# A four-layer graph network on one Trainium2 core: the score products of layer A in rounded halves, the column vectors of layer G by rows, and new steady sequences

## What is computed

```python
def layer_A(x, adj, Wq, Wk, Wv, Wo, bo):          # L0: masked attention, 4 heads of 64
    q, k, v = heads(x @ Wq), heads(x @ Wk), heads(x @ Wv)
    sim = where(adj, (q @ k.T) * 64 ** -0.5, -max)
    return merge(softmax(sim) @ v) @ Wo + bo
def layer_G(h, adj, W, bW, attn, A_w, ...):       # L1: 4 heads of 256
    Wh = h @ W[head].T + bW[head]
    scores = (Wh @ attn[head]) @ Wh.T
    hp = relu(tanh(where(adj, scores, 0)) @ Wh)
    ha, hf = concat(hp) @ A_w.T, h @ fc_w.T
    c = sigmoid(hf @ g1_w.T + ha @ g2_w.T + gbias)
    return hf * c + ha * (1 - c)
layer_B = ...                                     # L2: 8 heads of 32, scores and cosines
layer_D = ...                                     # L3: the same form as layer_A
x = norm(x + A(x)); x = norm(x + G(x)); x = norm(x + B(x)); x = norm(x + D(x))
```

## Time and profile before

| | |
|---|---|
| runs | 2783.31, 2783.71, 2779.02 us; median 2783.31 |
| profiled execution, its own time | 2784.76 us |
| its span | 2782.9 us |
| mean granted TensorE clock | 0.982 |
| share of the span that PE, DVE, ACT, POOL are busy | 96%, 71%, 50%, 33% |
| DMA | 29.77 MB, mean 11 GB/s |

### The profile page before, as it was taken

The page is one execution under the profiler, slowest core; times in us unless marked ns, Lnnn a source line. Parts: engine busy times, 40 slices in busy tenths (PEclk is TensorE's granted clock), DMA queues, the critical chain, the costliest instruction groups (busy, mean ns, idle before and its releaser), DMA issues.

```text
span 2782.9 us, 62595 instructions
## 1 busy us (share of the span) xinstructions
PE 2662.1 (96%) x21777; PEld 2332.1 (84%) x21777; DVE 1972.8 (71%) x6629; ACT 1398.4 (50%) x3861; POOL 908.0 (33%) x979
## 2 busy tenths in 40 slices
PE   8799999999999999999999999999999999999985
PEld 7788888888888888888898888888888889888873
DVE  2367777778777767777777777777877777777764
ACT  1355445555454545544555545554554554554542
POOL 1223233432323333323343233333332434332331
PEclk8899999999999999999999999999999999999996
DMA  4000000000000000000000000000000000000000
GB/s 128 6 3 11 1 11 10 9 9 9 0 9 9 9 9 9 9 0 9 9 9 9 9 0 9 9 9 9 9 4 6 9 9 9 9 9 0 10 5 8
DMA packets 44481, 29.77 MB, mean 11 GB/s; under 512 B 21264, under 2 KB 44048, under 8 KB 44432
## 3 DMA queue, kind: packets, MB, share of 16 engines
q1 hardware_dynamic: 44432, 29.13, 3.6%
HBM read 20.73 MB, written 8.39 MB: 10 GB/s over the span
## 4 chain that ended last, share of the span: by engine, by line
PE 69%; DVE 21%; issue 5%; ACT 3%; DVEq 1%; POOL 0%; DMA 0%; SPq 0%; ACTq 0%; POOLq 0%
PE bank L247 13%; PE bank L249 12%; PE bank L248 12%; PE bank L246 9%; PE bank L1139 4%; PE bank L324 4%; PE bank L236 4%; PE bank L313 3%; PE bank L1121 3%; DVE b L420 2%; DVE x L170 2%; PE bank L1149 2%; DVE arena L420 2%; DVE b L463 2%; DVE l_st L158 2%
## 5 line engine op out<-in xcount | busy, mean ns | idle before, releaser
L1533 POOL TENSOR_TENSOR arena_r<-a,arena_r 128x512 fp32r<-128x512 f32 x128 | 166.0, 1297 | 585.0 <-ACT arena_r L1229 585.0
L1279 ACT ACTIVATE b<-b,s_sh 128x256 f32<-128x256 f32 x512 | 253.7, 499 | 116.0 <-DVE s_sh L420 116.0
L178 POOL TENSOR_SCALAR l_ve<-l_mv 128x2 f32<-128x2 f32 x128 | 29.0, 227 | 864.2 <-DVE l_mv L163 861.8
L247 PE MATMUL bank<-arena_r 128*128 128x256 f32 x1024 | 301.4, 294 | 1.8 <-POOL arena_r L1538 1.8
L248 PE MATMUL bank<-arena_r 128*128 128x256 f32 x1024 | 289.8, 283 | 0.0
L249 PE MATMUL bank<-arena_r 128*128 128x256 f32 x1024 | 289.5, 283 | 0.0
L1538 POOL TENSOR_TENSOR arena_r<-a,arena_r 128x512 fp32r<-128x512 f32 x128 | 165.5, 1293 | 174.6 <-ACT arena_r L1223 172.1
L247 PEld LDWEIGHTS bank<-arena_r 128*128 128x128 f32 x1024 | 195.6, 191 | 22.5 <-issue 20.6
L420 DVE CUSTOM_DVE_ANT_0 b<-bank,s_add 128x256 f32<-128x256 f32 x512 | 183.4, 419 | 39.9 <-PE bank L1121 39.0
L1439 DVE SCALAR_TENSOR_TENSOR b<-bank,b 128x256 f32<-128x256 f32 x512 | 185.1, 416 | 20.3 <-PE bank L1130 20.0
L249 PEld LDWEIGHTS bank<-arena_r 128*128 128x128 f32 x1024 | 196.1, 191 | 0.0
(11 more groups left out here) (273 smaller groups left out, 9099.4 us busy)
## 6 DMA issues: line engine op xcount, KB each, us to landing
x_in<-in_x SPq DMA_DIRECT2D x32, 256.0 KB, 2.8
out<-x SPq DMA_DIRECT2D x32, 256.0 KB, 2.1
adj_a<-in_adj SPq DMA_DIRECT2D x32, 64.0 KB, 2.5
adj_b<-in_adj SPq DMA_DIRECT2D x32, 64.0 KB, 2.4
a<-in_L_gnn_W SPq DMA_DIRECT2D x4, 256.0 KB, 3.3
b<-in_L_gnn_A_w SPq DMA_DIRECT2D x1, 1024.0 KB, 7.1
arena<-in_L_gnn_attn SPq DMA_DIRECT2D x4, 256.0 KB, 7.2
g_b_wh<-in_L_gnn_bW SPq DMA_DIRECT2D x1, 512.0 KB, 9.2
```

The costliest lines, as they stand in the source:

```text
L247: pe.matmul(out, w[0], x[0], start=first, stop=False)
L1279: last = act.activation(S.e[:, n, it, :], S.e[:, n, it, :], ACT.Exp, bias=S.sh[:, it, h:h + 1], scale=-1.0, accum_out=S.sums[:, it, h:h + 1])
L1533: pool.tensor_tensor(G.wh[h % 2][1], G.whf[:, h % 2, :, :], G.wh[h % 2][0].bitcast(F32), ALU.subtract).then_inc(G.wh_sb.sem, 1)
```

## The change

Four things change.

1. **Scores of A.** q and k of A become pairs of rounded halves: ACT writes the upper halves (signals `q_hi`, `k_hi`), and DVE gets two new stages, `a_q` and `a_k`, for the lower ones. The scores become three products each. D keeps its plain products. A's k moves to places 20 and 21 of the arena.
2. **Column vectors of G.** `g_c` is now four products with eight weight columns (upper and lower half of `w_c` beside each other) and 256 moving columns, which give eight rows. ACT copies these rows (a new ACT stage `g_c`), and a new PE stage `g_c_t` turns them by two fp32 products with a small matrix `sel`, which also adds the halves. DVE's `g_c_t` then adds the bias as `g_c` did.
3. **Signals of the norms** are merged from four to two. The waits are the same.
4. **New sequences** for all four engines (the table `ORDER`).

```diff
@@ ORDER (all four lists are new; one line of each, for the form)
-        ("g_ha_3_1", 1), ("g_ha_3_0", 1), ("d_k", 2), ("g_ha_t", 1), ("a_x_t", 0), ("g_gate_x", 1), ("d_q", 2),
+        ("d_q", 2), ("d_k", 2), ("d_v", 2), ("d_scores_0", 2), ("d_scores_1", 2), ("a_q", 0), ("a_k", 0), ("a_v", 0),
@@ pe_attention, scores
         for it in range(T):
-            for half in range(2):
-                rows = slice(DHA * half, DHA * half + DHA)
-                last = pe.matmul(B[2 * pair + half][:, it * NODES:(it + 1) * NODES],
-                                 L.qt[rows, pair, it * P:(it + 1) * P], L.kt[rows, pair, :],
-                                 start=True, stop=True)
+            for n, (a, b) in enumerate(L.products):
+                for half in range(2):
+                    rows = slice(DHA * half, DHA * half + DHA)
+                    last = pe.matmul(B[2 * pair + half][:, it * NODES:(it + 1) * NODES],
+                                     L.qt[a][rows, pair, it * P:(it + 1) * P], L.kt[b][rows, pair, :],
+                                     start=(n == 0), stop=(n == len(L.products) - 1))
@@ act_attention, q (k likewise)
-        act.activation(L.qt[:, :, :], view(B[1]), ACT.Copy).then_inc(L.q_sb.sem, 1)
+        act.activation(L.qt[0], view(B[1]), ACT.Copy).then_inc((L.q_hi if L.fine else L.q_sb).sem, 1)
@@ dve_attention, new (k likewise)
+    def q(g):
+        dve.wait_ge(L.q_hi.sem, L.q_hi.at(g))
+        dve_lower(dve, B[1], L.qt).then_inc(L.q_sb.sem, 1)
@@ build
+        A.qt, A.kt = split(a32r, 14), split(a32r, 20)
+        A.products = (0, 0), (0, 1), (1, 0)
+        D.products = ((0, 0),)
@@ PE, g_c and the new g_c_t
             def g_c(g):
                 pe.wait_ge(G.x_t_sb.sem, G.x_t_sb.at(g))
+                for kc in range(T):
+                    for half in range(2):
+                        last = pe.matmul(BA[2][0:2 * HG, 0:NODES], G.w_c_rows[:, kc, :], G.xt[half][:, kc, :],
+                                         start=(kc == 0 and half == 0), stop=(kc == T - 1 and half == 1))
+                last.then_inc(G.c_psum.sem, 1)
+
+            def g_c_t(g):
+                pe.wait_ge(G.c_sb.sem, G.c_sb.at(g, 1))
                 for it in range(T):
-                    for kc in range(T):
-                        last = pe_product(pe, BA[2][:, it * HG:(it + 1) * HG],
-                                          part(G.xt, slice(None), kc, slice(it * P, (it + 1) * P)),
-                                          part(G.w_c, slice(None), kc), kc == 0, kc == T - 1)
+                    last = pe.matmul(BA[2][:, NODES + it * HG:NODES + (it + 1) * HG], G.c_rows[:, it * P:(it + 1) * P],
+                                     C.sel[:, :], start=True, stop=True)
                 last.then_inc(G.c_psum.sem, 1)
@@ ACT, new
+                elif stage == "g_c":
+                    act.wait_ge(G.c_psum.sem, G.c_psum.at(g, 1))
...
+                    act.activation(G.c_rows, BA[2][0:2 * HG, 0:NODES], ACT.Copy).then_inc(G.c_sb.sem, 1)
```

More of the change, by code:

```diff
@@ L65 @@
+        ("d_values_0", 2), ("d_values_1", 2), ("a_probs_0", 0), ("a_probs_1", 0), ("b_x_t", 1), ("a_probs_2", 0),
+        ("a_probs_3", 0), ("a_values_0", 0), ("a_values_1", 0), ("d_out", 2), ("a_out", 0), ("b_m", 1), ("b_q", 1),
+        ("b_k", 1), ("g_x_t", 0),
     ],
     "ACT": [
-        ("b_copy_6", 2), ("g_wh_3", 1), ("g_p_2", 1), ("g_s_3", 1), ("b_relu_1", 2), ("g_a_3", 1), ("g_p_3", 1),
-        ("d_x_t", 2), ("g_ha", 1), ("d_k", 2), ("g_ha_t", 1), ("a_x_t", 0), ("d_q", 2), ("g_gate", 1),
@@ L69 @@
-        ("d_exps_0", 2), ("a_k", 0), ("d_exps_1", 2), ("d_exps_2", 2), ("a_q", 0), ("d_exps_3", 2), ("d_probs_0", 2),
-        ("d_probs_2", 2), ("a_exps_0", 0), ("a_exps_1", 0), ("a_exps_2", 0), ("a_exps_3", 0), ("a_probs_0", 0),
-        ("b_x_t", 1), ("a_probs_2", 0), ("a_o_copy", 0), ("g_x_t", 0), ("b_k", 1), ("b_q", 1), ("g_z_0", 0),
[4 rows of a table removed]
+        ("g_x_t", 2), ("b_q", 3), ("b_k", 3), ("g_c", 2), ("g_z_0", 2), ("b_unit_t", 3), ("g_wh_0", 2),
[5 rows of a table added]
+        ("a_x_t", 1), ("g_gate", 2), ("d_k", 3), ("d_q", 3), ("d_exps_0", 3), ("d_exps_1", 3), ("a_q", 1),
@@ L76 @@
+        ("d_exps_2", 3), ("a_k", 1), ("d_exps_3", 3), ("d_probs_0", 3), ("a_exps_0", 1), ("a_exps_1", 1),
+        ("d_probs_2", 3), ("a_exps_2", 1), ("a_exps_3", 1), ("a_probs_0", 1), ("b_x_t", 2), ("a_probs_2", 1),
+        ("a_o_copy", 1),
     ],
     "DVE": [
-        ("b_factors", 2), ("b_copy_5", 2), ("b_copy_7", 2), ("g_p_2", 1), ("g_a_3", 1), ("b_scale", 2), ("b_sum", 2),
-        ("b_stats", 2), ("b_norm_out", 2), ("g_p_3", 1), ("g_diff", 1), ("a_x_t", 0), ("g_ha_t", 1), ("g_gate", 1),
@@ L80 @@
[L80 removed]
[3 rows of a table removed]
[L84 to L85 removed]
[5 rows of a table removed]
+        ("g_z_3", 2), ("g_p_1", 2), ("b_mask_4", 3), ("b_mask_5", 3), ("b_mask_6", 3), ("b_mask_7", 3), ("g_a_3", 2),
+        ("b_cut_4", 3), ("b_cut_5", 3), ("b_cut_6", 3), ("g_p_2", 2), ("b_cut_7", 3), ("b_copy_5", 3),
@@ new lines @@
+        ("b_factors", 3), ("b_copy_7", 3), ("g_p_3", 2), ("b_scale", 3), ("b_sum", 3), ("b_stats", 3), ("g_diff", 2),
+        ("b_norm_out", 3), ("g_ha_t", 2), ("g_gate", 2), ("g_mix", 2), ("g_sum", 2), ("g_stats", 2), ("a_x_t", 1),
[3 rows of a table added]
+        ("a_probs_1", 1), ("a_probs_3", 1), ("d_o_copy", 3), ("a_o_copy", 1), ("d_sum", 3), ("b_x_t", 2),
+        ("a_sum", 1), ("a_stats", 1), ("b_m", 2), ("a_norm_out", 1), ("b_square", 2), ("g_x_t", 1), ("g_wh_0", 1),
+        ("b_unit", 2), ("b_sem", 2), ("g_c_t", 1), ("g_z_0", 1), ("g_wh_1", 1), ("g_adj_t", 1), ("b_mask_0", 2),
[3 rows of a table added]
@@ L373, in k @@
         act.wait_ge(L.k_psum.sem, L.k_psum.at(g))
-        act.activation(L.kt[:, :, :], view(B[2]), ACT.Copy).then_inc(L.k_sb.sem, 1)
+        act.activation(L.kt[0], view(B[2]), ACT.Copy).then_inc((L.k_hi if L.fine else L.k_sb).sem, 1)
     def exps(g, h):
@@ L480, in slot @@
             x_t(g)
+        elif what == "q":
+            q(g)
+        elif what == "k":
+            k(g)
         elif what == "v":
@@ L1060, in slot_a @@
                     g_c(g)
+                elif stage == "g_c_t":
+                    g_c_t(g)
                 elif stage.startswith("g_s_"):
@@ L1379, in slot_a @@
                     g_z(g, int(stage[4:]))
-                elif stage == "g_c":
-                    dve.wait_ge(G.c_psum.sem, G.c_psum.at(g))
+                elif stage == "g_c_t":
+                    dve.wait_ge(G.c_psum.sem, G.c_psum.all(g))
                     if later(g):
```

76 lines of the change are left out of this document (40 added, 36 removed), and 35 rows, old and new, of the table ORDER.

## The result

The changed kernel takes 2798.76 us (median of five runs, 2795.32 to 2802.83) against 2783.31 for the kernel before (five runs, 2776.3 to 2784.34): ratio 1.0063, with a 95% interval of 1.0046 to 1.0079. It is slower by 0.6%. The forecast was 2745.

What follows compares the result with a forecast made beforehand. PE's work and waits for one graph bound the kernel, 82.4 us; 0.95 less work and 0.2 less waiting give 81.2, which over 32 graphs saves 38 us: 2745 us, range 2703 to 2787.

Steps and rivals of the forecast that it cites:

- The halves pair: A's scores on PE: 24 products run as twelve pairs, 1.7 instead of 2.5 us; no pairing had chance 0.08.
- D's two scores: On PE, D's two blocks of scores now touch and should take 2.0 to 2.2 us together.
- The wait before D's first values: In the heads, PE was to wait 0.9 us for DVE's copy of d_probs_1, behind two masks of A.
- The waits in the heads: PE's waits in the heads of D and A: 1.8 to 2.0 us a graph, against 1.75 before.
- The column vectors: G's column vectors on PE: two visits of 0.9 and 0.85 us instead of 1.33, so 0.4 more work.
- the 0.4 of entering and leaving: Cost in us of entering and leaving a tiled block on PE, worked out from a block of scores of 1.26.
- The wait before `g_p_3`: Outside the heads, a new PE wait of 0.35 us for POOL, where g_a_3 stands behind b_sums.
- the 0.3 for unknown ones: Allowance of 0.3 us a graph for unknown new PE waits outside the heads.
- Outside the heads: Step on PE's other waits: those before g_x_t (0.35) and b_transpose_4 (0.5) go; 0.35 and 0.3 are new.
- if PE waits at a place in the G and B stretch that I have without a wait: One of the signs named in advance that would show the forecast wrong; no size given.
- DVE's chain gets longer: Rival, chance 0.14: A's scores wait for both lower halves; 1.7 us more waiting a graph gives 2800 us.
- the touching blocks: A's two tiled score blocks on PE now touch, with one entry and exit, 0.3 us with the pause between.

Runs made afterwards that it cites:

- both: Changed kernel with 64 empty instructions ahead of DVE's set-up, and POOL's g_x_ha waiting until DVE has normalised B: 2721.68 us, ratio 0.9784 to the kernel before.
- plain: "both" with A's scores as one plain fp32 product again, without DVE's a_q and a_k: 2710.58 us, ratio 0.9738 to the kernel before.
- bpad: The kernel before with 92 empty instructions ahead of DVE's set-up, its loop unchanged: 2854.87 us, ratio 1.0266.
- probs1: "both" with DVE's copy d_probs_1 moved ahead of a_mask_0 and a_mask_1: 2750.54 us, ratio 0.9887 to the kernel before.

## Why the prediction was wrong

**What held.** The halves pair (a block of 1.62, forecast 1.6 to 1.8). D's two scores cost 2.08 together (2.0 to 2.2). The wait before D's first values was forecast at 0.9 and is 1.11, for the copy named. D's first transposes wait for nothing. DVE takes 15.4 from D's first mask to A's last copy but one in "both" (15 to 16). The waits in the heads, forecast at 2.0 in all, are 2.0 in "both" when read from its starts (1.1 before D's first values, 0.3 before the second, 0.3 before A's transposes, 0.3 smaller).

**What was mis-sized.** The column vectors: 0.9 and 0.85 forecast, 0.49 and 0.53 measured. I charged each visit the 0.4 of entering and leaving that I had worked out for a block of scores, and the small products do not pay it; only the second visit slows the starts around it, by 0.2 in all. The wait before `g_p_3` (0.35) is not there, nor the 0.3 for unknown ones, in "both". Together that is 1.4 too much; 0.6 that I counted too low takes part of it back, since "both" is at 80.4 and the forecast at 81.2. The 0.2 around the second visit are part of these 0.6; where the rest lies is not settled.

**What failed.** The step is "Outside the heads: ... New: `g_p_3` waits 0.35 ... I take 0.3 for unknown ones". Waits of 1.3 and 1.3 stand outside the heads, one in the stretch of G and B, one at its end: 81.2 and 1.3 and 1.3, less the 0.8, is 83.0. The text named "if PE waits at a place in the G and B stretch that I have without a wait" as what would make it wrong, and gave no mechanism for it.

The rival *DVE's chain gets longer* gave 2800, and 2798.76 came out. That is luck. Its place, A's scores behind the lower halves, costs PE 0.1 there ("plain" has it 0.12 shorter), and the time was lost elsewhere, by other causes.

Behind this are two assumptions that the text never states. One is that an instruction's duration is a property of the instruction. I took DVE's and POOL's from rows and laid the stages in a new order; but L169 takes 0.41 or 1.37 by what POOL does beside it. The trace of before shows it (timeline, all engines):

```profile
1093.58 1.29 POOL L1538 TENSOR_TENSOR arena_r<-a,arena_r 128x512 fp32r<-128x512 f32 x1
...
1094.32 1.98 DVE L170 TENSOR_SCALAR x<-x,l_mv,l_rs 128x256 f32<-128x256 f32 x2
1094.83 1.32 POOL L1533 TENSOR_TENSOR arena_r<-a,arena_r 128x512 fp32r<-128x512 f32 x1
```

There the slow normalisation was D's, for which nobody waited. The new order put the collision on B's, for which PE waits. The other assumption is that the start of a pass costs nothing wherever a list begins. It costs nothing on DVE before, and 75.1 us of idle time after, because of where the loop fell in the code. Neither is a cost of the new score products or column vectors themselves. The collision comes from the new sequences, and the loop's place from the amount of code ahead of it and in it. With both put right, order and new parts come out at 2721.68, better than the forecast.

**The halves of A's scores.** Priced on PE alone (0.8, of which the touching blocks are a part), they looked like a gain. Against the plain product in the same order they save PE 0.31, cost DVE 1.38, and lose 11 us in all.

## What to carry to other kernels

When a list is reordered, look for each stage on the critical chain at what the other engines run at that moment, and take its duration from rows with the same neighbour: a group whose mean (0.60) is far above its shortest member (0.41) tells that neighbours matter. Before an order is judged, see whether an engine idles on "issue" at its loop's start and whether the instruction queue moves packets in the steady state; 64 empty instructions in the set-up made this kernel 1.3% faster, and 92 made the one before 2.7% slower. When a run gives PE a longer wait, read the granted clock behind it: in "bpad" and "probs1" about a third of the loss was the clock and not the wait. A wait that is released by a copy is not cured by moving the copy before it is known what stands behind the wait.

## What the runs showed of the hardware that was not expected

- A loop of 296 or 300 instructions on DVE runs without a fetch at one place in the code and fetches five packets of 8 KB in each pass at another. The first register instruction of a pass then comes 2.9 to 3.4 us after the branch instead of 0.3. DVE idles 2.7 to 2.8 of it in the changed kernel, and 1.15 in "bpad", where it had more work in hand.
- A fetch is about 128 instructions on q14: in "bpad" they come at records 24, 153 and 279 of a pass.
- A single-source fp32 normalisation on DVE, 0.41 alone, stands until a two-source operation of POOL that began before it ends, up to 1.37. So does a small two-source one of 128x16: 0.99 instead of 0.16. Beside a single-source operation of POOL (uint8 to bf16) it took 0.40 when that had begun 0.7 before.
- Products with 8 weight columns, and with a contraction over 8 rows, cost 0.49 and 0.53 for four. The second kind slows the starts before and behind it by 0.1 each.
- The granted clock is 0.98 in the mean in all runs but two, and 1.00 in all their steady passes. In "bpad" (mean 0.974) and "probs1" (0.978) it falls to 0.50 for 3.4 us, in 15 and in 9 passes, each time just behind a wait of PE of 1.95 or 1.96. In the steady passes of the other runs PE's longest wait is 1.30, and the clock never falls. A fall costs 1.1 us a graph in "probs1" and 1.6 in "bpad".
